# A projection step moved behind the second pair of maximum products in an attention loop

## The chip, the cores and the metric

The kernel runs on one core of a Trainium2 chip. The metric is the device time of one execution in microseconds (us). Engines are named as in the profile: PE is TensorE (matrix products), DVE is VectorE, ACT is ScalarE, POOL is GpSimd, SP issues transfers. Each works through its own list of instructions in order, and they meet at semaphores.

## The reference

Two transformer-like layers over 4 batches of 512 tokens with 256 features, 16 heads of 16 features. What matters here is the softmax attention of the first layer and the projections that follow it:

```
q, k, v = x @ Wq.T, x @ Wk.T, x @ Wv.T          # q and k then rotated
scores  = einsum('bhqd,bhkd->bhqk', q, k) * scale
attn    = einsum('bhqk,bhkd->bhqd', softmax(scores), v)
combined = g * mem_out + (1 - g) * attn          # mem_out: a linear attention
x = x + combined @ Wo.T + ffn0(xn)
xn = layernorm(x)
q1, k1, v1 = silu(xn @ Wq1), silu(xn @ Wk1), silu(xn @ Wv1)
gate = (xn @ Wg1) @ Wg2                          # and router logits of layer 1
```

## The kernel before

The program has three stages with a barrier between them: `layer0_front` (projections and expert layer of layer 0), `middle` (softmax attention of layer 0, and the projections that open layer 1) and `layer1_main`. The change is in `middle`, on PE.

`middle` goes through batch `b`, group `g` of four heads, and tile `k` of 128 keys; one such `(g, k)` is called a slot here, and slots are numbered 4g + k, 0 to 15 in a batch. In one slot PE issues, in this order:

- the score products of heads 0 and 1 (`scores(k, (0, 1))`, L1426, into the two buffers `psE`); ACT reads each with an exponential (L1090);
- in slots with k = 1 four small transposes (`turn_max`, L1415), of row maxima for the next group;
- the maximum products of heads 0 and 1 (`rows`, L1408, into the two buffers `psM`). They compute the scores of the group two ahead in the transposed layout, and DVE takes the maximum of each row from them (`reduce`, L1180). The text calls them maximum products, and L1180 a reduction;
- the value products of the slot before (`values(k - 1)`, L1435), which read what ACT wrote;
- the score products of heads 2 and 3;
- a projection step, if this slot has one (`beside(k)`), and the maximum products of heads 2 and 3. It is these two that trade places.

At the end of a group PE issues the last value products, and DVE copies their result (`outT`, L1210) before it begins the next group's reductions. `psM` and `psE` have two buffers each, one for even and one for odd heads. So a maximum product of head 2 waits for the reduction of head 0 of the same slot, and that of head 0 of the next slot for the reduction of head 2. Score products wait in the same way for exponentials.

The projection steps belong to the batch before. PE, DVE, ACT, POOL and SP each have a table of steps by slot. On PE: slots 0 to 3 `heads(t)` (L1474, L1477), 4 `turn_combined` (L1487), 5 `project_out` (L1494), 8 `turn_x` (L1502), 9 `project_half(0)` (L58 to L60), 10 `logits_low`, 11 `turn_low`, 12 `project_half(1)`, 13 `project_gate` (L1546), 14 and 15 `project_tokens` (L58 to L60); slots 6 and 7 have none. Batch 0 runs without steps; batches 1 and 2 are a hardware loop with steps; in batch 3 only slots 0 to 7 have maximum products, as there is no later batch. Steps that go with maximum products are thus 14 + 14 + 6 = 34.

On the other engines a slot's step stands behind that slot's reductions (DVE) or exponentials (ACT): DVE weighs what `heads(t)` gave with three instructions (L1219, L1221, L1224) in slots 0 to 3; POOL then adds; ACT copies `turn_combined` and `turn_x` results (L1097, L1101), and applies silu to `project_half` (L1107) and sigmoid or silu to the last three. The functions of ACT sit in tables, so such a step has a table load before it and one behind it, ahead of the next exponential.

Of the kernel before, what the change touches and what calls it, by code (L numbers as in the profile page):

```python
# [755 lines left out]
def middle(nc, io, scratch, keep):  # L756
# [8 lines left out]
    with ExitStack() as ctx:  # L765
# [635 lines left out]
        def _(pe):  # L1401
            def rows(n, g, t, b, heads):

                if t == 0 and heads[0] == 0:
                    pe.wait_ge(stack_in[g], LOADED * (b + 1))
                for h in heads:
                    pe.wait_ge(rows_used[h % 2], 8 * n + 2 * t + h // 2)
                    nc.tensor.matmul(psM[:, h % 2, :], qst[g][0:STACK, h, t * P:(t + 1) * P], kst[g][0:STACK, h, :],  # L1408
                                     start=True, stop=True).then_inc(rows_ready, 1)

            def turn_max(n, i):
                pe.wait_ge(negmax_parts, n + 1)
                pe.wait_ge(nmT_copied, n)
                for t in range(TILES):
                    mm = nc.tensor.transpose(psN[0:2 * HG, t * P:(t + 1) * P],  # L1415
                                             nmparts[i][:, t, :, :].rearrange("p a h -> p (a h)"), identb[:, :])
                mm.then_inc(nmT_ready, 1)

            def attend(b, g, last, beside):
                G = GROUPS * b + g  # L1420
                pe.wait_ge(max_in[g], 16 * b + 16)

                def scores(k, heads):
                    for h in heads:
                        pe.wait_ge(scores_used[h % 2], 2 * (TILES * G + k) + h // 2)
                        nc.tensor.matmul(psE[h % 2][:, :], kst[g][0:STACKM, h, k * P:(k + 1) * P],  # L1426
                                         qst[g][0:STACKM, h, :], start=True, stop=True).then_inc(scores_ready, 1)

                def values(k):
                    for used in scores_used:  # L1430
                        pe.wait_ge(used, 2 * (TILES * G + k + 1))
                    if k == 0:
                        pe.wait_ge(out_copied, G)
                    for h in range(HG):
                        mm = nc.tensor.matmul(psV[VW * h:VW * (h + 1), :], vst[g][:, k, VW * h:VW * (h + 1)],  # L1435
                                              probs[k % PSLOTS][:, h, :], start=k == 0, stop=k == TILES - 1,
                                              tile_position=(0, VW * h), skip_group_check=True)
                    mm.then_inc(probs_used, 1)

                for k in range(TILES):  # L1440
                    ahead = not (last and g >= GROUPS - 2)
                    next_rows = G + 2, (g + 2) % GROUPS, k, b if g < 2 else b + 1
                    scores(k, (0, 1))
                    if k == 1 and not (last and g == GROUPS - 1):
                        turn_max(G + 1, (g + 1) % 2)
                    if ahead:
                        rows(*next_rows, (0, 1))
                    if k:
                        values(k - 1)
                    scores(k, (2, 3))  # L1450
                    beside(k)
                    if ahead:
                        rows(*next_rows, (2, 3))
                values(TILES - 1)


# [141 lines left out]
            def ready():  # L1598
                pe.wait_ge(consts_in, CONSTS)
                pe.wait_ge(weights_in, WEIGHTS)  # L1600
                pe.wait_ge(w_lo, 3)

            loop(pe, attend, {0: (heads(0),), 1: (heads(1),), 2: (heads(2),), 3: (heads(3),), 4: (turn_combined,), 5: (project_out,),
                              8: (turn_x,), 9: (project_half(0),), 10: (logits_low,), 11: (turn_low,), 12: (project_half(1),),
                              13: (project_gate,), "rank": (rank,), "invert": (invert,), 14: (project_tokens(0, gate_done, kk_ps),),
# [552 lines left out]
```

## Time and profile before

| | |
|---|---|
| median of three runs | 1091.43 us (1089.68 to 1092.42) |
| profiled execution, its own time | 1091.52 us, with a span of 1089.6 us |
| busy, share of the span | PE 946.9 us (87%), DVE 588.4 us (54%), ACT 433.1 us (40%), POOL 314.5 us (29%) |
| batch 1 with its steps | 398.5 to 494.9 us of the span |
| batch 2 with its steps | 494.9 to 590.3 us |
| slots of batch 3 that have steps and maximum products | 590.3 to 632.3 us |
| mean granted TensorE clock | 0.92 of full speed |

PE's busy time is modelled, and its rows overlap: a product row shows when it was issued and how long it took to run through, so the distance from one row to the next is what it cost.

### The profile page before, as it was taken

What the parts mean: (1) busy time and instruction counts of PE and PEld (TensorE: products, weight loads), DVE (VectorE), ACT (ScalarE), POOL (GpSimd) and SP (SyncE); (2) the same over time, 40 slices, a digit from 0 to 9 for tenths busy, and PEclk for the clock granted to TensorE, in tenths of its full rate; (3) what the DMA queues carried; (4) which work ended last, traced back from release to release, by engine and by line L of the source; (5) the groups of instructions that cost most, each with busy time, mean ns of one, the idle gap of its engine ahead of it and who ended that gap; (6) DMA issues with size and microseconds to landing.
All of it is one profiled execution on the core that took longest, in us unless ns stands there. A gap on an engine that the chain in (4) does not pass through costs nothing. (4 is left out here: it accounts for less than half of the span.)

```text
span 1089.6 us, 16172 instructions
## 1 busy us (share of the span) xinstructions
PE 946.9 (87%) x5323; PEld 614.9 (56%) x5323; DVE 588.4 (54%) x1218; ACT 433.1 (40%) x663; POOL 314.5 (29%) x218
## 2 busy tenths in 40 slices
PE   3789999999858999998999988575999999999991
PEld 2678888888711234453445445463666666666660
DVE  4556655563268767647755741474443443443435
ACT  3335536353234554674576467041222222222220
POOL 3632515225233000211021020143333433433321
PEclk9999999999957989888998988786999999999995
DMA  5622414033051221133233112628873433433316
GB/s 200 217 96 60 165 58 144 19 97 126 1 166 58 92 79 60 59 107 131 92 101 118 55 59 99 161 106 298 241 234 86 122 104 88 118 106 97 98 43 236
DMA packets 149836, 125.26 MB, mean 115 GB/s; under 512 B 63232, under 2 KB 127504, under 8 KB 149776
## 3 DMA queue, kind: packets, MB, share of 16 engines
q1 hardware_dynamic: 146032, 114.25, 33.9%
q0 software_dynamic: 3744, 10.23, 2.7%
q8 instruction: 35, 0.57, 0.2%
q14 instruction: 25, 0.20, 0.1%
HBM read 85.56 MB, written 38.86 MB: 114 GB/s over the span
## 5 line engine op out<-in xcount | busy, mean ns | idle before, releaser
L1180 DVE TENSOR_REDUCE b_negmax<-b_psM 128x1 f32<-128x512 f32 x256 | 163.2, 683 | 82.1 <-PE b_psM L1408 79.1
L1090 ACT ACTIVATE b_probs<-b_psE 128x512 f32<-128x512 f32 x256 | 138.8, 595 | 122.8 <-PE b_psE L1426 121.8
L1408 PE MATMUL b_psM<-b_kst,b_qst 96*128 96x512 bf16 x256 | 98.9, 433 | 27.9 <-DVE b_negmax L1180 14.0
L1426 PE MATMUL b_psE<-b_qst,b_kst 98*128 98x512 bf16 x256 | 90.0, 412 | 15.1 <-ACT b_probs L1090 10.5
L402 POOL TENSOR_TENSOR a_hh<-a_h,a_hh 128x512 fp32r<-128x512 f32 x44 | 57.8, 1313 | 144.7 <-ACT a_hh L455 144.7
L1426 PEld LDWEIGHTS b_psE<-b_qst,b_kst 98*128 98x128 bf16 x256 | 21.0, 100 | 109.6 <-ACT b_probs L1090 54.1
L1435 PE MATMUL b_psV<-b_probs,b_vst 128*32 128x512 f32 x512 | 75.9, 667 | 3.1 <-ACT b_probs L1090 3.1
L1928 PE MATMUL d_psG<-d_w,d_xT 128*128 x156 | 76.5, 614 | 2.2 <-DVE d_xT L1827 1.9
L1776 POOL DMA_INDIRECT scratch_ys<-d_y,put x39 | 39.7, 1017 | 129.2 <-ACT d_y L1808 127.8
L1953 PE MATMUL d_psY<-d_w,d_hidden 128*128 x312 | 74.9, 383 | 0.0
L1936 PE MATMUL d_psU<-d_w,d_xT 128*128 x156 | 74.5, 600 | 0.0
L1408 PEld LDWEIGHTS b_psM<-b_kst,b_qst 96*128 96x128 bf16 x256 | 24.3, 100 | 83.6 <-DVE b_negmax L1180 60.1
L1837 DVE TENSOR_TENSOR d_probs<-d_ps,decay 128x512 f32<-128x512 f32 x64 | 43.6, 687 | 47.0 <-PE d_ps L1971 46.9
L528 DVE TENSOR_TENSOR a_h<-a_h,a_psG 128x512 f32<-128x512 f32 x44 | 30.2, 686 | 67.8 <-ACT a_h L452 67.8
L1953 PEld LDWEIGHTS d_psY<-d_w,d_hidden 128*128 128x128 f32 x312 | 57.6, 190 | 12.9 <-issue 6.8
L1808 ACT ACTIVATE d_y<-d_psY 128x256 f32<-128x256 f32 x39 | 14.9, 383 | 122.1 <-PE d_psY L1953 122.1
L1782 POOL TENSOR_TENSOR d_rs<-d_ss,d_neghalf 128x16 f32<-128x16 f32 x16 | 46.9, 2933 | 56.4 <-DVE d_ss L1866 56.4
L1032 POOL TENSOR_TENSOR b_combined<-b_both 128x256 f32<-128x256 f32 x16 | 11.6, 727 | 173.6 <-DVE b_both L1224 173.6
L1832 DVE TENSOR_TENSOR d_hidden<-d_hidden,d_psU 128x512 f32<-128x512 f32 x39 | 26.8, 687 | 59.8 <-PE d_psU L1936 59.8
L1796 ACT ACTIVATE d_hidden<-d_psG 128x512 f32<-128x512 f32 x39 | 23.3, 597 | 85.7 <-PE d_psG L1928 85.7
L455 ACT ACTIVATE a_hh<-a_h 128x512 fp32r<-128x512 f32 x44 | 27.8, 633 | 73.8 <-DVE a_h L533 73.8
L58 PE MATMUL a_psO<-a_wd,a_hh 128*128 128x256 f32 x176 | 50.1, 285 | 1.3 <-POOL a_hh L402 1.3
(314 smaller groups left out, 2125.5 us busy)
## 6 DMA issues: line engine op xcount, KB each, us to landing
scratch_parts<-a_part SPq DMA_DIRECT2D x12, 512.0 KB, 4.3
b_qst<-scratch_parts SPq DMA_DIRECT2D x96, 64.0 KB, 2.1
b_kst<-scratch_parts SPq DMA_DIRECT2D x96, 64.0 KB, 2.1
scratch_parts<-b_part SPq DMA_DIRECT2D x24, 256.0 KB, 3.4
chunk_qst<-scratch_parts SPq DMA_DIRECT2D x96, 64.0 KB, 2.9
chunk_kst<-scratch_parts SPq DMA_DIRECT2D x96, 64.0 KB, 2.2
a_cbc<-scratch_cT SPq DMA_DIRECT2D x16, 256.0 KB, 3.9
scratch_v<-a_v SPq DMA_DIRECT2D x4, 1024.0 KB, 4.4
```

Of the source, the lines that this page charges most:

```text
L58: nc.tensor.matmul(out, ah, bh, start=start and i == 0, stop=False, skip_group_check=True)
L402: nc.gpsimd.tensor_tensor(hh[s % HSLOTS][1][:, :], h[s % 2][:, :], hh[s % HSLOTS][0][:, :].bitcast(F32), ALU.subtract).then_inc(lo_done, 1)
L1090: nc.scalar.activation(probs[k % PSLOTS][:, h, :], psE[h % 2][:, :], ACT.Exp, scale=float(HD) ** -0.5).then_inc(scores_used[h % 2], 1)
L1180: nc.vector.tensor_reduce(negmax[i][:, t, h:h + 1], psM[:, h % 2, :], AX_X, ALU.max, negate=True).then_inc(rows_used[h % 2], 1)
L1408: nc.tensor.matmul(psM[:, h % 2, :], qst[g][0:STACK, h, t * P:(t + 1) * P], kst[g][0:STACK, h, :], start=True, stop=True).then_inc(rows_re ...
L1426: nc.tensor.matmul(psE[h % 2][:, :], kst[g][0:STACKM, h, k * P:(k + 1) * P], qst[g][0:STACKM, h, :], start=True, stop=True).then_inc(score ...
L1435: mm = nc.tensor.matmul(psV[VW * h:VW * (h + 1), :], vst[g][:, k, VW * h:VW * (h + 1)], probs[k % PSLOTS][:, h, :], start=k == 0, stop=k = ...
L1782: nc.gpsimd.tensor_tensor(rs[:, :], ss[:, :], neghalf[:, :], ALU.pow).then_inc(rs_done, 1)
L1837: nc.vector.tensor_tensor(probs[g][:, :], (ps1 if g % 2 else ps0)[:, :], decay[:, HG * g:HG * g + HG, :].rearrange("p h c -> p (h c)"), AL ...
L1928: mm = nc.tensor.matmul(psG[:, :], xT[b % 2][:, k, :], weights(b, GATE + k * H1, H1), start=k == 0, stop=k == KT - 1)
L1936: mm = nc.tensor.matmul(psU[:, :], xT[b % 2][:, k, :], weights(b, UP + k * H1, H1), start=k == 0, stop=k == KT - 1)
L1953: mm = nc.tensor.matmul(psY[:, 0:D], hT[b % 2][:, k, :], weights(b, DOWN + k * D, D), start=k == 0, stop=k == HT1 - 1)
```

## The change

The step is issued behind the maximum products of heads 2 and 3 instead of ahead of them. Nothing is added or removed, and the lists of DVE, ACT, POOL and SP are the same.

```diff
@@ -1448,9 +1448,9 @@
                     if k:
                         values(k - 1)
                     scores(k, (2, 3))
-                    beside(k)
                     if ahead:
                         rows(*next_rows, (2, 3))
+                    beside(k)
                 values(TILES - 1)
```

On PE, slot 1 of the loop over batches 1 and 2 (L1426 scores, L1408 maximum products, L1474 and L1477 the step `heads(1)`):

```order
 L1426 MATMUL b_psE<-b_qst,b_kst 128x512 x2
+L1407 REGISTER_ALU
+L1408 MATMUL b_psM<-b_kst,b_qst 128x512 x2
 L1465 ISA
 L1474 MATMUL b_psX<-b_sel,b_outT 128x68 x4
 L1477 MATMUL b_psX<-mem,b_qf 128x136 x2
-L1407 REGISTER_ALU
-L1408 MATMUL b_psM<-b_kst,b_qst 128x512 x2
 L1425 ISA
 L1426 MATMUL b_psE<-b_qst,b_kst 128x512 x2
```

The two maximum products, with the instruction that sets up their wait, went ahead of the step's six products, and the next slot's scores now follow the step directly.

On PE, slot 8 of the same loop (L1502 is the step `turn_x`):

```order
 L1425 REGISTER_ALU
 L1426 MATMUL b_psE<-b_qst,b_kst 128x512 x2
+L1407 REGISTER_ALU
+L1408 MATMUL b_psM<-b_kst,b_qst 128x512 x2
 L1502 MATMUL b_psX<-ident,b_combined 128x128 x8
-L1407 REGISTER_ALU
-L1408 MATMUL b_psM<-b_kst,b_qst 128x512 x2
 L1425 ISA
 L1426 MATMUL b_psE<-b_qst,b_kst 128x512 x2
```

The same move, in the first slot of a group: what stands behind the maximum products on PE is now the step that ACT waits for.

## Rows read from the trace of the kernel before

**Rows 1.** Windows: busy us (instructions) of PE, PEld, DVE, ACT, POOL; PEclk, DMA share, GB/s

```profile
494.90:538.40 43.50, 40.48 (x216) 18.51 (x216) 31.98 (x69) 18.45 (x34) 3.92 (x5) 0.92 0.34 112
538.40:590.30 51.90, 47.92 (x247) 23.83 (x245) 30.21 (x68) 37.83 (x51) 8.75 (x4) 0.90 0.28 89
590.30:632.30 42.00, 38.53 (x215) 17.93 (x216) 31.42 (x67) 18.84 (x34) 3.91 (x5) 0.96 0.26 88
```

**Rows 2.** Line L1408, 397 to 633: idle of PE before it, us and times

```profile
  DVE b_negmax L1180: 39.5, 89
```

**Rows 3.** Timeline, batch 2, slots 2 and 3 (start us, us, engine, line)

```profile
506.19 1.07 PE L1435 MATMUL b_psV<-b_probs,b_vst 128*32 128x512 f32 x8
...
507.63 1.01 PE L1474 MATMUL b_psX<-b_sel,b_outT 128*128 128x68 f32 x8
...
508.99 0.60 PE L1408 MATMUL b_psM<-b_kst,b_qst 96*128 96x512 bf16 x2
509.40 1.29 DVE L1180 TENSOR_REDUCE b_negmax<-b_psM 128x1 f32<-128x512 f32 x2 [1.19 <-PE b_psM L1408]
509.42 0.60 PE L1426 MATMUL b_psE<-b_qst,b_kst 98*128 98x512 bf16 x2
...
510.61 0.35 DVE L1219 RECIPROCAL b_scale<-b_psX 128x32 f32<-128x32 f32 x1
510.75 0.39 PE L1408 MATMUL b_psM<-b_kst,b_qst 96*128 96x512 bf16 x1 [0.21 <-DVE b_negmax L1180]
...
511.07 1.07 PE L1435 MATMUL b_psV<-b_probs,b_vst 128*32 128x512 f32 x8
...
511.82 1.28 DVE L1180 TENSOR_REDUCE b_negmax<-b_psM 128x1 f32<-128x512 f32 x2
```

**Rows 4.** Timeline, batch 2, slots 0, 4 and 5

```profile
494.90 1.38 PE L1474 MATMUL b_psX<-b_sel,b_outT 128*128 128x68 f32 x8 [0.57 <-DVE b_outT L1210]
...
517.65 1.09 PE L1487 MATMUL b_psX<-ident,b_combined 128*128 128x128 f32 x8 [0.30 <-POOL b_combined L1032]
...
519.48 0.39 PE L1408 MATMUL b_psM<-b_kst,b_qst 96*128 96x512 bf16 x1 [0.21 <-DVE b_negmax L1180]
...
526.42 0.59 PE L1426 MATMUL b_psE<-b_qst,b_kst 98*128 98x512 bf16 x2
...
528.07 1.06 PE L1435 MATMUL b_psV<-b_probs,b_vst 128*32 128x512 f32 x8
```

**Rows 5.** Timeline, batch 2, slots 8 and 9

```profile
537.53 1.04 PE L1502 MATMUL b_psX<-ident,b_combined 128*128 128x128 f32 x8
537.68 2.47 DVE L1180 TENSOR_REDUCE b_negmax<-b_psM 128x1 f32<-128x512 f32 x4
538.42 0.39 PE L1408 MATMUL b_psM<-b_kst,b_qst 96*128 96x512 bf16 x1
...
539.01 0.39 PE L1408 MATMUL b_psM<-b_kst,b_qst 96*128 96x512 bf16 x1 [0.20 <-DVE b_negmax L1180]
...
541.73 1.26 DVE L1180 TENSOR_REDUCE b_negmax<-b_psM 128x1 f32<-128x512 f32 x2
541.87 0.59 PE L58 MATMUL b_psX<-b_xT,b_wqk 128*128 128x512 f32 x1
...
545.00 1.02 ACT L1107 ACTIVATE b_half<-b_psX 128x1024 f32<-128x1024 f32 x1 [0.57 <-PE b_psX L60]
```

**Rows 6.** Timeline, batch 2, slot 12 and the scores of slot 13

```profile
560.11 0.53 PE L58 MATMUL b_psX<-b_xT,b_wqk 128*128 128x512 f32 x1
...
560.82 1.28 DVE L1180 TENSOR_REDUCE b_negmax<-b_psM 128x1 f32<-128x512 f32 x2
...
563.17 1.02 ACT L1107 ACTIVATE b_half<-b_psX 128x1024 f32<-128x1024 f32 x1 [0.84 <-PE b_psX L60]
...
...
566.16 0.88 PE L1426 MATMUL b_psE<-b_qst,b_kst 98*128 98x512 bf16 x2
```

**Rows 7.** Windows: a stretch at the lower clock in slots 14 and 15

```profile
570.70:577.40 6.70, 6.50 (x26) 3.86 (x27) 1.89 (x3) 5.42 (x7) 2.13 (x1) 0.50 0.50 170
```

## The prediction

> **What bounds the kernel now.** I read the stages by windows first. Only the three stretches in which steps run beside attention are touched. In the half of a batch with slots 0 to 7 PE is busy 40.48 of 43.50 us, DVE only 31.98 and ACT 18.45 (in batch 3 PE 38.53 of 42.00). In the half with slots 8 to 15 it is PE 47.92 of 51.90, DVE 30.21 and ACT 37.83 [rows 1]. No engine is full there; each waits for another inside a slot. So the question is not who is busiest but which wait ends last, slot by slot.
>
> The waits around the moved products came next. Between 397 and 633 us PE stood idle ahead of maximum products until a reduction was done: 39.5 us in 89 waits [rows 2]. This counts weight loads and products alike and is partly hidden behind products that still run, so it is a list of places and no amount to win.
>
> Then the timeline, from which I take four rules. A maximum product may use its buffer again 0.74 us after the reduction of it began (537.68 to 538.42), the next one 0.60 later (to 539.01) [rows 5]. A pair of products takes 0.43 (508.99 to 509.42), and DVE begins on it 0.41 after it was issued [rows 3].
>
> In slot 2 the step `heads(2)` runs from 507.63 to 508.99. Only then come the maximum products of heads 2 and 3, so DVE idles 1.19 before their reductions. The first pair of slot 3 is in turn held by these: the values stand at 511.07, where the scores at 509.42 and two free pairs would have put them at 509.42 + 0.86 = 510.28 [rows 3]. That is 0.79 us a slot of which the change can get hold.
>
> In slots 8 and 12 it is otherwise. They open a group, DVE is late there, and the maximum products of heads 2 and 3 are held by the first reductions. Today the step is issued ahead of this wait and runs inside it: `turn_x` at 537.53, the held products at 538.42 and 539.01 [rows 5]. In slot 12 the step stands at 560.11, ahead of reductions that begin at 560.82 [rows 6].
>
> **The change, term by term.** It adds no work and no transfer, and no other engine's list changes. In each of 34 steps two products of 0.43 us go ahead of the step. Behind them on PE stand the step, then the next scores; who waits for these is DVE, POOL or ACT. I follow batch 2 and count in us at PE.
>
> *Slots 0 to 7, gains.* Slot 0: the step waits for DVE's copy (494.90, idle 0.57) [rows 4], and the products now fill this wait; DVE also comes to its copy earlier relative to PE, as the second reductions of slot 15 no longer queue behind that slot's step. Estimate 0.6; 0.3 in batch 1, where no step came before. Slot 1: the first pair of slot 2 is no longer held, 0.79.
>
> Slots 2 and 3: the products now wait ahead of the step, because DVE reaches the first reductions late. The new ring is: step end, 0.2 to 0.4 until DVE sees it, 1.21 for three DVE instructions (510.61 to 511.82), 0.74 + 0.60 until the second product may go, 0.22 for it, 1.36 for the step; together 4.33 to 4.53, against 4.88 from values to values now (506.19 to 511.07) [rows 3]. Gain 0.35 to 0.55, I take 0.45 once. Slot 3 gives back some 0.25: the group's last values follow the step directly, so its wait counts in full.
>
> Slot 4: `turn_combined`, 0.87 us of the eight transposes that also make up `turn_x`, ran inside a wait (517.65, held products until 519.48) [rows 4] and becomes exposed. Against it, DVE's work ahead of these reductions no longer queues behind slot 3's late ones and comes some 0.9 earlier. I take zero; the bounds are 0.9 lost and 0.3 won. Slot 5: as slot 1; values 528.07 against 526.42 + 0.86 [rows 4], 0.79.
>
> Sum: 0.6 + 0.79 + 0.45 - 0.25 + 0 + 0.79 = 2.4 a batch, 2.1 in batch 1; over three batches 6.9 us gained. Bounds for a batch: 1.5 and 2.8.
>
> *Slots 8 to 15, losses.* Slot 8: the held products stay where they are, and the step follows at 539.01 + 0.22 = 539.23, not 537.53. ACT gets its input 1.70 later and the next scores come 0.87 later. Slot 9: reductions at 541.73 + 0.87 = 542.60, second product at 543.94, step at 544.16; it began at 541.87, and the silu behind it at 545.00 [rows 5] comes about 2.2 later. Slot 9 is bound by ACT: table load, silu, table load, exponentials, and then only scores. So slot 10's second scores are 2.2 late. The unheld first pair of slot 11 gives back 0.79, which leaves 1.4.
>
> Slot 12: DVE's reductions at 560.82 + 1.4 = 562.2, second product 563.55, step 563.8 against 560.11: about 3.5 late (its first products ran up slowly). The silu at 563.17 and, behind the table load, the scores at 566.16 go along [rows 6]. Slots 13 to 15 are the same ring of ACT; each step is 0.43 later for its products, which the unheld first pairs and idle ACT time mostly return: I take 0.3 for the three.
>
> Sum: 3.8 a batch, in batches 1 and 2 alone: 7.6 us lost. Lower bound 2.6: six steps on ACT's ring by 0.43, if DVE is never late. Upper bound 5.0, if in slot 14 DVE is held by a transfer on top.
>
> *Total:* 7.6 - 6.9 = +0.7 us. To the profiled execution, 1091.52, this gives 1092.2; that execution stands 0.1 above the median shown, so 1092.1 for a median. The terms' bounds give 2 x 2.6 - 3 x 2.8 = -3.2 and 2 x 5.0 - 3 x 1.5 = +5.5.
>
> *The clock* is the term that I can't place. From 570.7 to 577.4 the granted clock is 0.50, that is 1.2 GHz, and PE is busy 6.50 of 6.70 us [rows 7]; it fell after slots with waits on ACT. At full clock this work would take half, so one such stretch more or less is worth up to 3.3 us. The Trainium skill ("TensorE: Matmul & The Clock Gate", section "A second HAM failure mode: psum-queue depth-cycling") tells of a kernel that cycles through PSUM banks and leaves TensorE idle so often for a moment between groups that its clock swings between the two rates. That speaks against a change that puts waits into slots 8 to 15; that the clock falls there already agrees with it, and the sum above holds it unchanged.
>
> **Rivals.**
>
> A, *slower by the clock.* The added waits of 1 to 2 us ahead of steps in slots 9 and 12 bring another low stretch in each of the two batches. For it: the half with slots 8 to 15 already has the lower clock of the two, 0.90 against 0.92 [rows 1]. Against it: in slots 0 to 7 waits disappear. One stretch gives 1092.2 + 3.3 = 1095.5, two 1098.8. It decides from one full stretch on, +2.6. The page's rule would come out as this.
>
> B, *faster: the steps of slots 8 and 12 are not held.* If DVE, which leads by 2.4 us after slot 5, still leads PE at slot 8, the held products go before the old 538.42, and only 0.43 a step is lost. For it: DVE idles 1.19 in slot 2 and more elsewhere. Against it: slots 6 and 7 carry the longest DVE steps, and their products are held throughout, so DVE and PE shift together. With 2.6 lost it is 5.2 - 6.9 = -1.7, 1089.8. It decides below 1088.2, which needs a loss of at most 1.8 a batch, or the low stretch of [rows 7] gone as well (1086.5).
>
> C, *the wait merely changes its place.* Every reduction still takes 0.60, and if each first pair's wait comes back ahead of the step, nothing moves: 1091.5. For it: the ring of slots 2 and 3 shows just that for half of the gain. Against it: slots 1 and 5.
>
> **How the numbers follow.** A measurement of this kernel tells about 0.3% (3.3 us) from no change. My forecast, gains and losses that nearly cancel, has 0.50, and C 0.12; both lie within that bound. A has 0.25 and ends above it; B with its clock has 0.13 and ends below it. So faster 0.13, same 0.62, slower 0.25. Alone, the forecast reaches from 1088.3 to 1097.0 by its terms. The range takes one low stretch into account upward and B downward: 1088.0 to 1097.5.
>
> **What would show it.** Right: in slots 2 and 6 the first pair goes straight behind its scores, with no idle for a reduction; values to values in slots 2 and 3 is near 4.4; the stretch of slots 0 to 7 is about 2 us shorter; `turn_x` and `project_half` stand behind held products, and the half with slots 8 to 15 is 3 to 4 us longer. Wrong: `turn_x` within 0.6 us of its second scores (then B), or another number of low stretches between 397 and 633 us (then A, or luck in the clock).

## The result, and the profile after

| | before | after |
|---|---|---|
| first measurement, median | 1091.93 us (4 runs, 1089.68 to 1095.97) | 1103.23 us (4 runs, 1095.33 to 1106.93) |
| median of all runs whose clock is on record | 1092.12 us (81 runs of the three later measurements) | 1099.65 us (22 runs, 1090.30 to 1106.93, with the first four) |
| profiled execution, its own time | 1091.52 us | 1095.33 us, with a span of 1093.5 us |
| mean granted clock of that execution | 0.920 | 0.919 |

The ratio of the first measurement is 1.0095, 95% interval 1.0053 to 1.0136; of two later ones of the same kernel 1.0057 (1.0033 to 1.0081) and 1.0089 (1.0062 to 1.0116). The change makes the kernel slower, by 0.6 to 0.95%. The forecast was no change, 1092.1 us.

**One kernel, many times.** The 22 runs of the changed kernel spread over 17 us, and they order themselves by the clock: 1090.30 us at 0.924, 1106.93 us at 0.907. To work with this I turn each run's mean clock into its *low time*: 2 x (1 - clock) x span, the time spent at 1.2 GHz if the rest was at 2.4. For the 81 runs of before it lies between 165 and 193 us (median 179), for the 22 of after between 165 and 206 (median 191). Within every kernel of this study a us of low time goes with about 0.35 us of time (0.34 for before, 0.37 for after, correlations 0.91 and 0.97). So each kernel gets two numbers: its median time, and its mean time with every run brought to a low time of 180 us by that slope, called *the time at equal clock*. Before: 1091.9. After: 1096.2. So 4.3 us of the loss are there at equal clock, and 12 us more of low time add 12 x 0.35 = 4.2. Together that is 8.5, where the medians differ by 7.5. (The means differ by 8.1; their low times are 179.1 and 189.9, and 10.8 x 0.35 = 3.8 goes with 4.3 to 8.1.) The profiled executions have nearly the same clock (low times 174 and 177), so their difference of 3.8 us shows mostly the first part.

**Where these 3.8 us are.** Windows from the first value products of a slot to those of another. Kernel before, batch 1 slot 0 to slot 7, to slot 15, then batch 2 slots 0, 7 and 15, then batch 3 slots 0 and 7 (columns as in [rows 1]):

```profile
403.22:438.33 35.11, 32.24 (x174) 14.56 (x173) 25.35 (x53) 15.13 (x27) 3.92 (x5) 0.95 0.19 56
438.33:490.31 51.98, 49.80 (x254) 25.04 (x253) 29.49 (x71) 36.33 (x50) 8.74 (x4) 0.87 0.27 87
490.31:500.41 10.10, 8.32 (x37) 3.67 (x37) 7.56 (x14) 5.21 (x8) 0.00 (x0) 0.76 0.40 121
500.41:534.74 34.33, 31.46 (x173) 14.00 (x173) 25.35 (x53) 15.13 (x27) 3.92 (x5) 0.97 0.32 110
534.74:585.84 51.10, 48.58 (x254) 24.64 (x253) 29.41 (x71) 36.33 (x50) 8.75 (x4) 0.90 0.27 88
585.84:595.15 9.31, 7.71 (x37) 3.49 (x36) 7.17 (x13) 5.21 (x8) 0.00 (x0) 0.82 0.33 102
595.15:628.56 33.41, 30.57 (x174) 13.75 (x173) 25.72 (x55) 15.13 (x27) 3.91 (x5) 1.00 0.26 92
```

The same seven windows of the changed kernel:

```profile
403.45:435.64 32.19, 30.03 (x173) 13.87 (x172) 25.72 (x53) 15.03 (x27) 3.92 (x5) 0.99 0.22 61
435.64:494.11 58.47, 50.87 (x254) 25.93 (x253) 33.55 (x74) 35.88 (x49) 8.73 (x4) 0.85 0.25 78
494.11:502.48 8.37, 7.16 (x38) 3.13 (x37) 4.86 (x11) 5.56 (x8) 0.00 (x0) 0.82 0.34 98
502.48:534.48 32.00, 30.03 (x173) 13.86 (x172) 25.78 (x53) 15.03 (x27) 3.92 (x5) 0.99 0.39 131
534.48:590.47 55.99, 48.26 (x254) 24.16 (x253) 33.42 (x74) 35.87 (x49) 8.72 (x4) 0.91 0.26 80
590.47:600.08 9.61, 8.13 (x38) 4.04 (x37) 4.86 (x11) 5.56 (x8) 0.00 (x0) 0.74 0.34 98
600.08:632.48 32.40, 30.56 (x173) 13.76 (x172) 25.78 (x53) 15.02 (x27) 3.92 (x5) 0.97 0.28 95
```

Slots 0 to 7 are shorter in each batch, by 2.92, 2.33 and 1.01 us; slots 8 to 15 are longer, by 6.49 and 4.89; the passage from slot 15 to slot 0 is 1.73 shorter once and 0.30 longer once. With the 0.23 by which the first window starts later this sums to +3.92, all of the difference of the spans (3.9). The signs are those of the prediction, which had about 2 us shorter for the first half and 3 to 4 us longer for the second.

**The first half does what was foreseen.** Timeline of the changed kernel, batch 2, slots 2 and 3:

```profile
506.15 0.60 PE L1426 MATMUL b_psE<-b_qst,b_kst 98*128 98x512 bf16 x2
...
506.58 0.60 PE L1408 MATMUL b_psM<-b_kst,b_qst 96*128 96x512 bf16 x2
...
507.11 1.07 PE L1435 MATMUL b_psV<-b_probs,b_vst 128*32 128x512 f32 x8
507.58 2.68 DVE L1180 TENSOR_REDUCE b_negmax<-b_psM 128x1 f32<-128x512 f32 x4
...
509.14 1.01 PE L1474 MATMUL b_psX<-b_sel,b_outT 128*128 128x68 f32 x8
...
511.46 1.07 PE L1435 MATMUL b_psV<-b_probs,b_vst 128*32 128x512 f32 x8
```

The first pair goes 0.43 behind its scores with no wait, DVE reduces four times without a gap where it had idled 1.19 [rows 3], and the step comes last. From values to values it is 4.35 (forecast 4.33 to 4.53).

**The second half has a surprise.** Timeline of the changed kernel at slot 12 of batch 2, with POOL, DVE and PE:

```profile
559.55 2.12 POOL L1055 TENSOR_TENSOR b_part<-b_half,b_part 128x1024 bf16<-128x1024 f32 x1 [5.05 <-ACT b_part L1125]
...
559.81 1.89 DVE L1188 CAST b_nmparts<-b_negmax 128x16 bf16<-128x16 f32 x1
...
562.44 2.47 DVE L1180 TENSOR_REDUCE b_negmax<-b_psM 128x1 f32<-128x512 f32 x4
...
563.18 0.39 PE L1408 MATMUL b_psM<-b_kst,b_qst 96*128 96x512 bf16 x1 [1.55 <-DVE b_negmax L1180]
...
563.77 0.39 PE L1408 MATMUL b_psM<-b_kst,b_qst 96*128 96x512 bf16 x1 [0.21 <-DVE b_negmax L1180]
...
563.87 0.52 PE L58 MATMUL b_psX<-b_xT,b_wqk 128*128 128x512 f32 x1
```

The reductions and the step stand where the forecast put them (562.2 and 563.8). But DVE is late for a reason that the forecast did not name: its cast of 16 elements a partition (L1188), which prepares the next maxima, takes 1.89 us, and ends at 561.70, when POOL's subtraction (L1055) does, at 561.67. The median of the eight such casts between 398 and 600 us is 0.17. PE waits 1.55 us, with nothing to do. And the step that follows runs slowly. Windows of the changed kernel, 4.6 us from the step's first product on, batches 2 and 1:

```profile
563.87:568.47 4.60, 4.60 (x14) 3.46 (x14) 1.04 (x2) 0.00 (x0) 0.00 (x0) 0.63 0.48 141
465.15:469.75 4.60, 4.60 (x14) 3.45 (x14) 1.04 (x2) 0.00 (x0) 0.00 (x0) 0.63 0.48 142
```

From its first product to its last the step takes 4.23 us (563.87 to 568.10) in both batches; in the kernel before the change it took 2.64 in batch 2 (560.11 to 562.75), and the granted clock was 1.00.

### The profile page after: what moved, and what is told of

Its sections match the earlier page's. It is cut to its first block and busy times, and to the rows that moved or that the text cites. A ratio compares the mean times of both kernels' runs of the same rounds, so it can differ in the third digit from the quotient of the medians.

```text
span 1093.5 us, 16172 instructions
## 1 busy us (share of the span) xinstructions
PE 944.3 (86%) x5323; PEld 615.0 (56%) x5323; DVE 592.3 (54%) x1218; ACT 432.6 (40%) x663; POOL 314.4 (29%) x218
## 5 line engine op out<-in xcount | busy, mean ns | idle before, releaser
L1408 PE MATMUL b_psM<-b_kst,b_qst 96*128 96x512 bf16 x256 | 97.3, 431 | 29.7 <-DVE b_negmax L1180 18.3
L1426 PE MATMUL b_psE<-b_qst,b_kst 98*128 98x512 bf16 x256 | 89.6, 409 | 22.1 <-ACT b_probs L1090 17.7
L1426 PEld LDWEIGHTS b_psE<-b_qst,b_kst 98*128 98x128 bf16 x256 | 20.1, 99 | 111.8 <-ACT b_probs L1090 67.8
L1408 PEld LDWEIGHTS b_psM<-b_kst,b_qst 96*128 96x128 bf16 x256 | 24.6, 100 | 84.1 <-DVE b_negmax L1180 55.6
L1032 POOL TENSOR_TENSOR b_combined<-b_both 128x256 f32<-128x256 f32 x16 | 11.6, 727 | 168.7 <-DVE b_both L1224 168.7
```

## The experiments

All but the repeats keep the new order for some slots only, or change one thing beside it. For the choice of slots the code of the changed kernel is this, and only the condition differs:

```diff
+                    late = <condition>
+                    if not late:
+                        beside(k)
                     if ahead:
                         rows(*next_rows, (2, 3))
-                    beside(k)
+                    if late:
+                        beside(k)
```

| kernel | new order in | runs | median us | ratio to before, 95% | low time, median | at equal clock |
|---|---|---|---|---|---|---|
| before | none | 81 | 1092.12 | | 179 | 1091.9 |
| after | all slots | 22 | 1099.65 | see above | 191 | 1096.2 |
| e2_first_half | 0 to 7 | 12 | 1088.74 | 0.9976 (0.9955 to 0.9997) | 183 | 1088.0 |
| e3_second_half | 8 to 15 | 6 | 1103.18 | 1.0113 (1.0085 to 1.0141) | 187 | 1100.7 |
| e4_selected | 0, 1, 2, 3, 5 | 6 | 1083.15 | 0.9927 (0.9904 to 0.9951) | 175 | 1084.8 |
| e5_no_openers | all but 4, 8, 12 | 12 | 1089.01 | 0.9969 (0.9950 to 0.9988) | 186 | 1087.0 |
| e6_openers | 4, 8, 12 | 5 | 1105.07 | 1.0137 (1.0096 to 1.0177) | 192 | 1100.5 |
| e7_third_later | all, POOL later | 12 | 1097.28 | 1.0051 (1.0027 to 1.0076) | 190 | 1093.3 |
| e8_more | 0, 1, 2, 3, 5, 10, 11 | 12 | 1087.02 | 0.9951 (0.9933 to 0.9969) | 180 | 1086.5 |
| e9_sel_third | as e4, POOL later | 12 | 1085.52 | 0.9939 (0.9918 to 0.9959) | 178 | 1085.5 |
| e10_filled | all, waits filled | 12 | 1097.18 | 1.0045 (1.0026 to 1.0064) | 183 | 1096.4 |
| e11_slot12 | 12 | 12 | 1096.59 | 1.0063 (1.0036 to 1.0090) | 184 | 1095.1 |

The standard error of a mean at equal clock is 0.1 (before) to 0.35. The three measurements of before, made beside these kernels on three chips, give 1091.8, 1092.0 and 1091.8 at equal clock, so the rows can be compared. The row of e6_openers leaves out a sixth run, 1113.58 us at a clock of 0.903; with it the median is 1105.11, and the time at equal clock 1100.6.

**e1_again: the changed kernel, unedited.**

> The changed kernel once more, for the spread of its runs and a second profile. Slot theory (slots 0 to 7 gain, slots 8 to 15 lose, all by waits that the first profile shows): every run near that profile's 1095.3, within 2 us, at a clock near 0.92. Clock theory (the waits ahead of steps bring more stretches at the lower clock, in some executions more than in others): 1095 to 1107 again, and the time rises as the granted clock falls from 0.92 to 0.907; the second profile, if slow, has more low stretches between 397 and 760 us.

Measured: 1099.38 us, ratio 1.0057 (1.0033 to 1.0081). At equal clock 1096.2, as in the first four runs (1096.4); those four had low clocks (0.907 to 0.919). The loss is real, and two things make it up.

**e2_first_half and e3_second_half: one half each.**

```diff
+                    late = g < 2        # e2_first_half
+                    late = g >= 2       # e3_second_half
```

> Step behind the maximum products in slots 0 to 7 only. Slot theory: the first profile's gains alone, about 7 us: 1085, with slots 8 to 15 as before. Clock theory: the same, at a clock of 0.92 or more, since this half has fewer waits. Rival, that any shift of the work against the clock's stretches costs time: 1091 to 1100, with runs spread as widely as those of the changed kernel.

> Step behind the maximum products in slots 8 to 15 only. Slot theory: the first profile's losses alone, 11 us: 1103, clock 0.915 to 0.92. Clock theory: 1103 to 1112, at clocks of 0.905 to 0.912. Rival, that any shift costs: 1091 to 1100, as with the other half.

Measured at equal clock: slots 0 to 7 gain 3.9 us (1091.9 - 1088.0), slots 8 to 15 lose 8.8 (1100.7 - 1091.9). The sum, +4.9, is close to the +4.3 of both together, so the halves hardly touch each other. The first half gains 3 us less than the forecast's 6.9; the second loses 1.2 more than its 7.6.

**e4_selected: the first half without slot 4.**

```diff
+                    late = TILES * g + k in (0, 1, 2, 3, 5)
```

> Step behind the maximum products in slots 0, 1, 2, 3 and 5 only; slot 4, a group's first, as before. Slot theory: as with all of slots 0 to 7, 1085, within 1.5 us of it, as slot 4 came out at about zero in the first profile (its step 0.9 exposed, DVE 0.9 earlier). If the held products of slot 4 cost something after all: 1 to 2 us faster than with all eight slots.

Measured: 1083.15 us, ratio 0.9927 (0.9904 to 0.9951), the fastest kernel of the study and faster than both given ones. At equal clock the five slots gain 7.1 us, and slot 4 takes 3.2 of that away (1088.0 - 1084.8), 1.07 in each of three batches. Slot 4 of batch 1 in the changed kernel (timeline; L1487 is the step):

```profile
418.69 2.47 DVE L1180 TENSOR_REDUCE b_negmax<-b_psM 128x1 f32<-128x512 f32 x4
...
419.42 0.39 PE L1408 MATMUL b_psM<-b_kst,b_qst 96*128 96x512 bf16 x1 [0.55 <-DVE b_negmax L1180]
...
420.02 0.39 PE L1408 MATMUL b_psM<-b_kst,b_qst 96*128 96x512 bf16 x1 [0.21 <-DVE b_negmax L1180]
...
420.24 1.04 PE L1487 MATMUL b_psX<-ident,b_combined 128*128 128x128 f32 x8
...
421.12 0.60 PE L1426 MATMUL b_psE<-b_qst,b_kst 98*128 98x512 bf16 x2
```

The same place in e4_selected (its L1491 is that step):

```profile
418.43 2.60 DVE L1180 TENSOR_REDUCE b_negmax<-b_psM 128x1 f32<-128x512 f32 x4
418.45 1.04 PE L1491 MATMUL b_psX<-ident,b_combined 128*128 128x128 f32 x8
...
419.32 0.83 PE L1408 MATMUL b_psM<-b_kst,b_qst 96*128 96x512 bf16 x2
...
419.99 0.60 PE L1426 MATMUL b_psE<-b_qst,b_kst 98*128 98x512 bf16 x2
```

From the reductions to the next scores it is 2.43 with the step behind the held products and 1.56 with the step ahead, 0.87 apart: the step's whole length. DVE begins about as early in both. That early start comes from slots 1 to 3, whichever way slot 4 is ordered.

**e5_no_openers and e6_openers: without and with the openers.** These are slots 4, 8 and 12, which open a group after the first.

```diff
+                    late = TILES * g + k not in (4, 8, 12)     # e5_no_openers
+                    late = TILES * g + k in (4, 8, 12)         # e6_openers
```

> Step behind the maximum products in every slot but 4, 8 and 12, the slots that open a group after the first. Theory that the openers carry the loss (their products are held by a DVE that is late after a group's end): the changed kernel at a low-clock time of 180 us is 1096.1; without slot 4 (3.1), slot 8 (2 x 0.9) and slot 12 (2 x 3.4) that is 1084. Theory that ACT's ring in slots 9 and 13 to 15 carries it: 1093 or more.

> Step behind the maximum products in slots 4, 8 and 12 only. Opener theory: 1091.8 + 3.1 + 1.8 + 6.8 = 1103, at a lower granted clock than before. Theory of ACT's ring: at most 1097.

Measured at equal clock: the openers alone lose 8.6 us, all other slots together gain 4.9. So three of fourteen slots make the change a loss, in the medians as well (1105.07 and 1089.01). Both numbers lie some 3 us from what was expected, 1100.5 against 1103 and 1087.0 against 1084. With 3.2 for slot 4 and 3.2 for slot 12 (e11_slot12, below) about 2.2 are left for slot 8, which was not measured alone. The other slots of the second half cost 2.2 over e4_selected (1087.0 - 1084.8).

**e7_third_later: POOL's subtraction waits until DVE's cast and the subtraction behind it are done.** It tests whether the long cast is what delays slot 12. PE's order is that of the changed kernel.

```diff
+                if not isinstance(n, int):
+                    pool.wait_ge(negmax_parts, 4 * n + 9)
                 pool.wait_ge(part_done[1], 2 * n + 1)
```

> The changed kernel, with POOL's subtraction of slot 12 made to wait in batches 1 and 2 until DVE has split the maxima at the end of the group. Theory that this subtraction holds up DVE's cast (2.0 us in the changed kernel, 0.9 before, 0.17 elsewhere) and so the products ahead of slot 12's step: cast 0.17, the step of slot 12 1.7 to 1.9 earlier in two batches, 3.5 us less than the changed kernel at equal clock, 1092 to 1093. Rival, that DVE is late for its copy of the last values anyway, or that POOL's later end delays slots 13 and 14: within 1 us of the changed kernel at equal clock.

The group of the cast (L1190 here) in e7_third_later between 398 and 600 us, with least, median and longest ns:

```profile
L1190 DVE CAST b_nmparts<-b_negmax x8: 152/166/171, 417.9 to 587.3; 128x16 bf16<-128x16 f32 x8
```

Timeline of e7_third_later, slot 12 of batch 1:

```profile
461.62 0.15 DVE L1190 CAST b_nmparts<-b_negmax 128x16 bf16<-128x16 f32 x1
...
462.06 2.13 POOL L1057 TENSOR_TENSOR b_part<-b_half,b_part 128x1024 bf16<-128x1024 f32 x1 [5.75 <-DVE b_nmparts L1192]
462.52 2.60 DVE L1182 TENSOR_REDUCE b_negmax<-b_psM 128x1 f32<-128x512 f32 x4
...
463.41 0.84 PE L1410 MATMUL b_psM<-b_kst,b_qst 96*128 96x512 bf16 x2
...
463.95 0.53 PE L58 MATMUL b_psX<-b_xT,b_wqk 128*128 128x512 f32 x1
```

Measured: all eight casts are short (the longest was 2.02 us in the changed kernel), PE's products go without the long wait, and at equal clock 2.9 us come back (1096.2 - 1093.3) in two batches, where 3.5 were expected. So in the changed kernel the held cast costs about as much as moving the step of slot 12 alone (3.2, e11_slot12). The low time stays high (190).

**e8_more: slots 10 and 11 added to e4_selected.** By the forecast the unheld first pair of slot 11 gives back 0.79 a batch.

```diff
+                    late = TILES * g + k in (0, 1, 2, 3, 5, 10, 11)
```

> As the selection of slots 0, 1, 2, 3 and 5, with slots 10 and 11 added. Slot theory: the first pair of slot 11 is no longer held, 0.8 in two batches, so 1.5 us under that selection, 1082 to 1083 at a low-clock time of 180 us. Ring theory (a step of 10 or 11 that comes 0.43 later delays ACT's ring at slot 12): the same or up to 1 us slower than the selection.

Measured: 1087.02 us, at equal clock 1.7 more than e4_selected. The 1.5 us that were expected back do not come; in two batches these two slots lose about 0.4 each, with a standard error of 0.1, which is what two more products (0.43) ahead of a step cost if all of it counts.

**e9_sel_third: e4_selected with POOL later as in e7.**

> The selection of slots 0, 1, 2, 3 and 5 with POOL's subtraction of slot 12 behind DVE's split of the maxima. Theory that the held cast (1.5 us in the selection's profile) matters only where a step stands behind the products it delays: the same as the selection, within 1 us at equal clock. Rival, that DVE's delay costs the selection too: 1 to 3 us faster, 1082 to 1084 at a low-clock time of 180 us.

Measured: 1085.5 at equal clock against 1084.8, medians 1085.52 and 1083.15: no gain. In e4_selected a cast is held too (the longest 1.59 us), but there slot 12's step stands ahead of the products that wait, and fills the time. A late DVE costs only where PE has nothing else to do.

**e11_slot12: slot 12 alone.**

```diff
+                    late = TILES * g + k == 12
```

> Step behind the maximum products in slot 12 only, two steps in all. Opener theory with the held cast: the step's products come 3.4 us later in each of two batches, 1092 + 6.8 = 1099 at a low-clock time of 180 us, if nothing gives it back. As forecast, without the cast: 2 us a batch, 1096.

Measured: 1096.59 us, ratio 1.0063 (1.0036 to 1.0090); 3.2 us lost at equal clock, by a single slot in two batches. That is nearer to the 4 us of the forecast's own path than to the 6.8 of the other theory, which took the long casts of the changed kernel for given. Here, with slots 8 to 11 as before, the casts of slot 12 took 1.29 and 0.75 us, against 2.02 and 1.89 there.

**e10_filled: useless products in PE's waits.** If PE's waits are what lowers the clock, filling them should bring the low time down and leave the time at equal clock alone. Ahead of the held products of slots 4, 8 and 12 PE issues 5, 8 and 15 products of 256 columns into an unused part of another buffer.

```diff
-        psN = ctx.enter_context(nc.psum_tensor("b_psN", [P, SEQ], BF16))
+        psN = ctx.enter_context(nc.psum_tensor("b_psN", [P, 2 * SEQ], BF16))
+        psD = psN[:, SEQ:2 * SEQ].bitcast(F32)
...
+                    if ahead and not (isinstance(b, int) and b == 0):
+                        for _ in range({4: 5, 8: 8, 12: 15}.get(TILES * g + k, 0)):
+                            nc.tensor.matmul(psD, kst[g][0:STACK, 0, k * P:(k + 1) * P],
+                                             qst[g][0:STACK, 0, 0:SEQ // 2], start=True, stop=True, skip_group_check=True)
                     if ahead:
                         rows(*next_rows, (2, 3))
                     beside(k)
```

> The changed kernel with small products of no use (256 columns, result read by nobody) ahead of the held products: 5 in slot 4, 8 in slot 8, 15 in slot 12, as many as fit into the waits that its profile shows. Theory that TensorE's waits in the openers bring the additional time at the lower clock: low-clock time falls from 190 us to about 181 as before the change, and the median from 1099.5 to 1096 or 1097. Rival, that the clock falls for what comes before or after these waits: low-clock time stays at 188 to 192 and the median at 1099 or more.

Timeline of e10_filled, slot 12 of batch 1 (L1454 are the added products):

```profile
460.83 2.02 DVE L1189 CAST b_nmparts<-b_negmax 128x16 bf16<-128x16 f32 x1
...
462.61 1.80 PE L1454 MATMUL b_psN<-b_qst,b_kst 96*128 96x256 bf16 x15
...
464.33 0.39 PE L1409 MATMUL b_psM<-b_kst,b_qst 96*128 96x512 bf16 x1
...
465.02 0.52 PE L58 MATMUL b_psX<-b_xT,b_wqk 128*128 128x512 f32 x1
```

Windows of e10_filled, 4.6 us from the step's first product on, batches 2 and 1:

```profile
560.28:564.88 4.60, 4.60 (x25) 2.79 (x28) 1.70 (x5) 1.51 (x2) 0.00 (x0) 1.00 0.50 140
465.02:469.62 4.60, 4.60 (x25) 2.79 (x28) 1.71 (x5) 1.51 (x2) 0.00 (x0) 1.00 0.48 142
```

Measured: the cast is held as before, but the wait is filled, and the step runs at clock 1.00 in both batches where the changed kernel's had 0.63. At equal clock nothing changed (1096.4 against 1096.2); the low time fell from 191 to 183 (means 189.9 and 180.3, with standard errors of 2.3 and 2.6) and the median to 1097.18. Adding work made the kernel faster by 2.5 us; the means differ by 3.2, with a standard error of 1.2.

**e12_third_time: the changed kernel again, on the same chip as e9 to e11.**

> The changed kernel beside the three others, as their measure on the same chip. Median 1098 to 1101, low-clock time 188 to 192 us, 1096 at a low-clock time of 180 us, as in 16 runs so far.

Measured: 1101.51 us, ratio 1.0089 (1.0062 to 1.0116), low time 196, at equal clock 1096.2. Against this median e10_filled is 4.3 us faster.

**All the profiles together.** In each, the time from the first to the last product of slot 12's step can be read twice. With the step behind the held products and the wait in place (the changed kernel three times, e3, e6, e11) it took 4.1 to 4.2 us in six of twelve cases and 2.6 in the other six. With the wait shortened (e7) or filled (e10), none of four was above 2.7; with the step ahead (before, e2, e4, e5, e8, e9), none of twelve. In the six slow cases PE had waited 1.51 to 1.56 us ahead of the held products, in the other six 0.32 to 1.20.

Whether such a slow step is additional low time is another question. In e12_third_time the step of batch 1 took 2.63 us and that of batch 2 4.24. Windows from 12 us before its first product to 30 behind it, batches 1 and 2:

```profile
454.21:496.21 42.00, 36.66 (x186) 17.88 (x186) 24.81 (x58) 28.39 (x38) 4.50 (x3) 0.87 0.24 79
547.94:589.94 42.00, 35.74 (x186) 18.06 (x185) 24.75 (x57) 27.41 (x37) 6.39 (x3) 0.88 0.22 73
```

The clock is the same, 0.87 and 0.88: around the slow step there was no more low time, but some of it fell on the step. Nor is there more of it in the changed slots as a whole. Windows of the stretch with the changed slots and of the 132 us behind it, in before, then e1_again, then e12_third_time:

```profile
397.00:633.00 236.00, 217.79 (x1145) 103.31 (x1149) 155.89 (x337) 134.55 (x207) 29.24 (x23) 0.91 0.27 88
633.00:765.00 132.00, 94.46 (x534) 65.40 (x532) 57.31 (x137) 51.73 (x65) 34.84 (x23) 0.79 0.47 154
397.00:633.00 236.00, 211.52 (x1116) 103.30 (x1114) 155.62 (x328) 131.23 (x201) 28.29 (x23) 0.91 0.28 88
633.00:765.00 132.00, 93.80 (x530) 65.56 (x531) 59.40 (x144) 53.50 (x68) 32.57 (x22) 0.76 0.41 132
397.00:633.00 236.00, 210.23 (x1146) 101.55 (x1150) 159.28 (x337) 134.17 (x207) 29.25 (x23) 0.93 0.27 88
633.00:765.00 132.00, 96.00 (x514) 66.72 (x511) 55.78 (x135) 50.71 (x63) 33.60 (x23) 0.74 0.44 144
```

The first profile of the changed kernel has 0.91 and 0.78. In the changed slots the clock is no lower than before in any of the three; behind them it is lower in all three. These are single executions, and e9_sel_third, whose low time is that of before, shows 0.74 behind them too. So the profiles do not show where the 12 us of low time lie.

## Why the prediction was wrong

The mechanism of the waits and both signs were right, and each place the forecast worked out stands near where it was put. What failed are two steps, and one term was small.

*Slots 0, 1, 2, 3 and 5: right.* Forecast 6.9 us gained, measured 7.1 for the five together (e4_selected). The ring of slots 2 and 3 came out at 4.35.

*Slot 4, "I take zero": the first step that failed.* It costs 3.2 us over three batches, 1.07 each; the lower bound of the forecast was 0.9 a batch. I had set the 0.87 us of the step, which loses its cover, against DVE's earlier start. But that start is a gain of slots 1 to 3; it comes whether or not slot 4 is changed, as the two timelines show. It was counted against a cost with which it has nothing to do.

*Slots 8 to 15: mechanism right, size 1.2 too small.* Forecast 7.6 us lost, measured 8.8 (e3_second_half). At the values of slot 7 the changed kernel stands only 0.26 earlier than the kernel before (534.48 against 534.74). With that added, `turn_x` began at 539.25 (forecast 539.23), `project_half(0)` at 543.98 (544.16), the reductions of slot 12 at 562.70 (562.2) and `project_half(1)` at 564.13 (563.8). The delay of 2.2 that was to shrink to 1.4 until slot 12 was 2.1 at the second scores of slot 10 (549.84 against 547.99) and 1.5 at the first scores of slot 12 (559.67 against 558.44). So slots 10 and 11 gave back in the changed kernel what the forecast said, though added to a kernel without that delay they cost (e8_more).

The held cast of slot 12 I did not foresee, and that the place came out is in part luck: the row from which it was counted, 560.82, stands behind a cast that POOL already held in the trace of before (0.94 us at 559.14, ending as POOL's subtraction does), so much of the hold was in the forecast without being named there. In the kernel before the step covers it. Which slot the 1.2 us belong to is not shown.

*The sum at equal clock* was +0.7 and is +4.3. Slot 4 (3.2) and the second half (1.2), less 0.2 in the first, bring it to 4.9, which is the sum of the two halves measured alone; the whole change has 0.6 less, which the standard errors allow.

*The clock, "the sum above holds it unchanged": the second step that failed, and as large.* The low time rose by 12 us, worth 4.2. Rival A had a rise, by a wait of 1 to 2 us ahead of a step, at 0.25, and priced it at 1095.5 or 1098.8; its number was the better forecast. Its place, one more low stretch in each of the two batches, is not what the profiles show: between 397 and 633 us the clock is 0.91 before and 0.91, 0.91 and 0.93 after. So that the number came near is in part luck. What is shown is that such a wait can put the step of slot 12 at the lower clock, which then takes 1.6 us more (4.23 against 2.64), and that PE's waits have a part in the rise, as filling those of the openers takes back 8 of the 12 us of low time. The Trainium skill's rule that was weighed there ("TensorE: Matmul & The Clock Gate", section "A second HAM failure mode: psum-queue depth-cycling"), that short idle moments between groups of products make the clock swing, agrees with e10_filled: with the wait filled the step of slot 12 ran at 1.00, without it at 0.63. That these waits are the whole cause is not shown. With the hold of slot 12 gone, e7_third_later still had 190 us, and with no opener moved at all, e5_no_openers had 186. The rest stays open.

*Rivals B and C* fell. DVE leads nowhere far enough for the products of slots 8 and 12 to be free (PE waited 0.72 in slot 8 and 1.55 in slot 12), and the waits of slots 1 to 3 and 5 did not come back elsewhere, as the 7.1 us of e4_selected show.

## What to carry to other kernels

Before moving a step behind a wait, ask of every single slot whether the step was the work that covered the wait: where it ran beside an idle stretch it was free, and the same move that gains 7 us in slots whose step delayed others loses 9 in three slots where it filled a gap. Do not set a cost that the move causes against a gain that another part of the change brings anyway; cost each slot as if it were the only one changed, and keep only the slots that win (here 0, 1, 2, 3 and 5: 0.9927, 0.9904 to 0.9951). Compare kernels at equal granted clock as well as by medians, and price a new wait of PE twice: for itself, and for the work behind it, which may run at the lower clock (here 1.6 us more on a step of 2.64, in six of twelve cases).

## What the hardware showed that was not expected

A cast of 128 x 16 elements on DVE takes 0.15 to 0.17 us, and up to 2.02 us while POOL subtracts 128 x 1024 elements in 2.12. In batch 2 of the changed kernel the cast began 0.26 us behind the subtraction and ended 0.03 behind it. The Trainium skill ("SBUF — State Buffer", section "Who interferes with whom") says that the two engines share a pair of ports, and that with a DVE instruction that uses this pair too, as a cast can, whichever begins first keeps the pair for its whole instruction; the trace agrees, to 0.03 us. The small subtraction behind the cast (L1190), 0.17 us elsewhere, took 0.72 in slot 4 of both kernels, beside an addition of POOL (L1032) that took 0.72 and had begun 0.04 us ahead of it. DVE's reductions of 0.60 to 0.68 us were not held by the subtraction that ran beside them in e7_third_later (four in 2.60 us, against 2.47 in slot 12 of the changed kernel).

The low time of one and the same kernel differs by 28 us (before, 81 runs) to 41 us (after, 22 runs) from execution to execution, which is 10 and 14 us of time.
